# Softmax division moved to tokens on partitions, in a transformer stack of four gated layers on one core

## The reference, cut to what matters

```python
for l in range(4):
    x = x + tanh(g_xattn[l]) * xattn_l(layernorm(x), ctx)
    x = x + tanh(g_ffn[l]) * ffn_l(layernorm(x))
# attention, as in every layer: H heads of width d
probs = softmax(q @ k.T * scale + bias)      # over 256 keys
out = (probs @ v) per head -> [tokens, 128]
y = out @ Wo
```

## Time and profile before

| | us |
| --- | --- |
| median of three runs | 1080.95 |
| lowest, highest | 1071.59, 1083.82 |
| the profiled execution | 1068.41 |
| its span, first to last instruction | 1066.7 |

### The profile page before, as it was taken

How to read it: one execution, slowest core, us unless ns; L and a number is a source line. 1 busy time by engine, 2 the same in 40 slices (tenths; PEclk the granted TensorE clock), 3 DMA queues, 4 the chain that set the end, 5 groups by cost and what they waited for, 6 DMA issues and landing times.

```text
span 1066.7 us, 19274 instructions
## 1 busy us (share of the span) xinstructions
PE 880.5 (83%) x7316; PEld 573.0 (54%) x7316; DVE 787.8 (74%) x1849; ACT 493.7 (46%) x753; POOL 302.4 (28%) x324
## 2 busy tenths in 40 slices
PE   1778787788899998887898877787888999998686
PEld 1533346454566676663465323564456667776443
DVE  3899998778666945449778999878779574554783
ACT  2655453345534532217874656234554343322475
POOL 3600246443443211100323023655335330110000
PEclk9999777698989999988999989677998999988899
DMA  9100000000000000000110000000000000000000
GB/s 322 33 2 2 2 1 1 1 2 2 2 1 2 2 1 6 6 1 2 42 32 21 2 2 1 1 1 2 3 3 1 1 2 1 1 1 1 2 7 17
DMA packets 11741, 14.26 MB, mean 13 GB/s; under 512 B 1604, under 2 KB 10716, under 8 KB 11396
## 3 DMA queue, kind: packets, MB, share of 16 engines
q1 hardware_dynamic: 11552, 12.88, 3.7%
q10 hardware_dynamic: 100, 0.14, 0.1%
HBM read 11.55 MB, written 1.05 MB: 12 GB/s over the span
## 4 chain that ended last, share of the span: by engine, by line
PE 43%; DVE 40%; ACT 7%; issue 6%; SPq 1%; DMA 1%; POOL 1%; DVEq 0%; ACTq 0%
PE banks L986 36%; DVE nm_row L1440 13%; DVE probs L1459 5%; PE pv L986 4%; ACT probs L943 2%; DVE qf_row L1470 2%; DVE wide L1529 2%; DVE st_row L1283 2%; PE banks L682 2%; DVE xn_row L1395 1%; DVE mv_row L1285 1%; DMA xn_row<-in_ctx 1%; ACT wide L965 1%; ACT qT_row L860 1%; ACT kT_row L860 1%
## 5 line engine op out<-in xcount | busy, mean ns | idle before, releaser
L1440 DVE TENSOR_REDUCE nm_row<-banks 128x4 f32<-128x1024 f32 (+1 forms) x192 | 210.3, 1128 | 39.2 <-PE banks L986 38.6
L776 POOL TENSOR_TENSOR rstd_row<-rstd_row,neghalf 128x2 f32<-128x2 f32 x66 | 47.6, 721 | 365.8 <-DVE rstd_row L1390 277.8
L943 ACT ACTIVATE probs<-banks 128x1024 f32<-128x1024 f32 (+1 forms) x144 | 128.2, 933 | 36.5 <-PE banks L986 35.9
L986 PE MATMUL banks<-wide,c 128*128 128x256 f32 x512 | 127.9, 406 | 0.0
L986 PE MATMUL banks<-qT_row,kT_row 50*128 50x256 bf16 (+2 forms) x896 | 89.9, 298 | 29.6 <-DVE nm_row L1440 15.6
L986 PE MATMUL pv<-probs,vpad 128*32 128x256 f32 (+1 forms) x1536 | 105.7, 395 | 9.8 <-ACT probs L938 6.6
L986 PE MATMUL banks<-kT_row,qT_row 48*128 48x256 bf16 (+2 forms) x896 | 92.3, 294 | 25.7 <-DVE nm_row L1440 15.7
L986 PEld LDWEIGHTS banks<-wide,c 128*128 128x128 f32 x512 | 101.0, 202 | 18.3 <-issue 0.9
L938 ACT ACTIVATE probs<-probs 128x1024 f32<-128x1024 f32 x64 | 67.5, 1056 | 50.0 <-DVE probs L1459 48.1
L986 PE MATMUL banks<-c,wide 128*128 128x128 f32 x512 | 85.4, 336 | 3.7 <-POOL wide L834 3.7
L986 PEld LDWEIGHTS banks<-c,wide 128*128 128x128 f32 x512 | 79.6, 245 | 8.1 <-issue 6.4
(11 more groups left out here) (220 smaller groups left out, 1585.5 us busy)
## 6 DMA issues: line engine op xcount, KB each, us to landing
c<-in_c SPq DMA_DIRECT2D x1, 2500.0 KB
wide<-in_mask SPq DMA_DIRECT2D x8, 256.0 KB, 2.9
qT_row<-mT_row SPq DMA_DIRECT2D x96, 4.0 KB
c<-in_c SPq DMA_DIRECT2D x1, 1194.5 KB
xn_row<-in_ctx SPq DMA_DIRECT2D x8, 128.0 KB, 3.5
x_row<-in_x SPq DMA_DIRECT2D x8, 128.0 KB, 2.4
late<-in_late SPq DMA_DIRECT2D x2, 512.0 KB, 15.4
out<-x_row SPq DMA_DIRECT2D x8, 128.0 KB, 2.0
```

Of the source, the lines that this page charges most:

```text
L776: return pool.tensor_tensor(t, t, neghalf[:, 0:n], ALU.pow)
L943: act.activation(dst[:, :, 0:w], src[:, :, 0:w], ACT.Exp, scale=1.0 if l == 2 else HD ** -0.5).then_inc(sem["probs"], 1)
L986: return pe.matmul(dst, lhsT, rhs, start=start, stop=stop, **kw)
L1440: V.tensor_reduce(nm[b][:, t, :, 2 * jp:2 * jp + 2], ps[:, :, :, 0:kn], AX.X, ALU.max, negate=True).then_inc(sem["max"], 1)
```

## The change

The division is done with tokens on partitions. In all four layers `o_flip` on TensorE becomes four f32 transposes of 128x128 (two token tiles t by two groups g) from `weighed_sb` into a bank o_ps. VectorE then inverts, with one token on each partition, only the sums themselves: 32 columns in the wide layers (16 heads for each of two tiles), 8 columns in layer 2, into a corner of the buffer qr. It multiplies with the inverse broadcast along the head: in the wide layers two products of 128 columns (one for each place of a head in its strip), in layer 2 one of 256 columns, into qf. A new step `o_turn` follows: TensorE transposes qf back (two transposes of 128x128), and ScalarE copies the 256 columns into oT. `mix` is as before. The matrix `spreads`, its memset, its eight copies, the wait on `setup_zero` and their part of `n_late` are gone. In the plan, the costs are new (`o_flip` PE .75 and DVE .8 for 1.03 and 2.13, `o_turn` PE .42 and ACT .27), and the eight `LEAD` values are others, so that the orders of all engines are planned anew. The diff, cut to its core:

```diff
@@ row_steps
-        out += [("divide", l, row), ("o_flip", l, row), ("mix", l, row)]
+        out += [("divide", l, row), ("o_flip", l, row), ("o_turn", l, row), ("mix", l, row)]
@@
-LEAD = [280.3, 290.2, 324.8, 314.7, 4.7, -4.1, 22.7, 13.6]
+LEAD = [277.9, 316.1, 319.2, 304.8, -11.0, -1.1, 7.7, 22.0]
@@ COST
-        "o_flip": [("PE", 1.03), ("DVE", 2.13)], ("o_flip", 2): [("DVE", 2.13)], "mix": [("PE", .5), ("DVE", .4)],
+        "o_flip": [("PE", .75), ("DVE", .8)], "o_turn": [("PE", .42), ("ACT", .27)], "mix": [("PE", .5), ("DVE", .4)],
@@ starts_after
-                "o_flip": [(of("divide", l), "ACT")], "mix": [(of("o_flip", l), "DVE")],
+                "o_flip": [(of("divide", l), "ACT")], "o_turn": [(of("o_flip", l), "DVE")], "mix": [(of("o_turn", l), "ACT")],
@@ psum_uses
-        "o_flip": [("oT_ps", "one", "oT")] if l != 2 else [],
+        "o_flip": [("o_ps", "one", "o_normed")], "o_turn": [("oT_ps", "one", "oT")],
@@ SP, step consts
-                        sp.wait_ge(setup_zero, 1)
-                        for j in range(2):
-                            for c in range(LANES):
-                                at_row, head = COLS * c + j * (HD + 1), LANES * j + c
-                                sp.dma_start(spreads[at_row:at_row + HD + 1, :], dram["spreads"][head * (HD + 1):(head + 1) * (HD + 1), 0:P]).then_inc(const_in, 16)
@@ ScalarE
+                    if kind == "o_turn":
+                        evac(oT[b][:, :], "oT_ps", bank("oT_ps", s)[:, 0:SEQ], "oT")
@@ TensorE
-                    if kind == "o_flip" and l != 2:
-
+                    if kind == "o_flip":
                         pe.wait_ge(sem["sums"], at("sums", s))
+                        claim(pe, "o_ps", s)
+                        for t in range(NT):
+                            for g in range(2):
+                                n = 2 * t + g
+                                ins = pe.transpose(bank("o_ps", s)[:, n * P:(n + 1) * P], weighed_sb[b][:, g, t * P:(t + 1) * P], ident)
+                        ins.then_inc(sem["o_ps"], 1)
+                    if kind == "o_turn":
+                        pe.wait_ge(sem["o_normed"], at("o_normed", s))
                         claim(pe, "oT_ps", s)
-                        for i, n in enumerate(("o", "r")):
-                            a, w = SPREAD_COLS[n]
-                            for g in range(2):
-                                ins = mm(bank("oT_ps", s)[g * w:(g + 1) * w, i * SEQ:(i + 1) * SEQ], spreads[:, a:a + w],
-                                         weighed_sb[b][:, g, :])
+                        for t in range(NT):
+                            ins = pe.transpose(bank("oT_ps", s)[:, t * P:(t + 1) * P], qf[b][:, t, :], ident)
                         ins.then_inc(sem["oT_ps"], 1)
@@ VectorE
                     if kind == "o_flip":
-                        over = qf[b][:, :, :].rearrange("p t d -> p (t d)")
+                        dve.wait_ge(sem["o_ps"], at("o_ps", s))
+                        ps = bank("o_ps", s)
                         if l == 2:
-                            dve.wait_ge(sem["sums"], at("sums", s))
-                            num, den = weighed_sb[b][:, 0, :], weighed_sb[b][:, 1, :]
+                            four = ps[:, :].rearrange("p (t n c d) -> p t n c d", t=NT, n=2, c=MQ)
+                            over = qr[b][:, 0, 0:NT * MQ].rearrange("p (t c) -> p t c", t=NT)
+                            ch.link(V.reciprocal(over, four[:, :, 1, :, 0]))
+                            V.tensor_tensor(qf[b][:, :, :].rearrange("p t (c d) -> p t c d", c=MQ), four[:, :, 0, :, :],
+                                            over[:, :, :, None].to_broadcast([P, NT, MQ, MD]), ALU.mult).then_inc(sem["o_normed"], 1)
                         else:
-                            dve.wait_ge(sem["oT_ps"], at("oT_ps", s))
-                            ps = bank("oT_ps", s)
-                            num, den = ps[:, 0:SEQ], ps[:, SEQ:2 * SEQ]
-                        ch.link(V.reciprocal(over, den))
-                        V.tensor_tensor(oT[b][:, :], num, over, ALU.mult).then_inc(sem["oT"], 1)
+                            strips = ps[:, :].rearrange("p (n c w) -> p n c w", n=2 * NT, c=LANES)
+                            over = qr[b][:, 0, 0:NT * HEADS].rearrange("p (n c j) -> p n c j", n=2 * NT, c=LANES)
+                            dst = qf[b][:, :, :].rearrange("p t (g j c d) -> p (t g) j c d", g=2, j=2, c=LANES)
+                            ch.link(V.reciprocal(over, strips[:, :, :, HD:2 * HD + 2:HD + 1]))
+                            for j in range(2):
+                                n = j * (HD + 1)
+                                ins = V.tensor_tensor(dst[:, :, j, :, :], strips[:, :, :, n:n + HD],
+                                                      over[:, :, :, j, None].to_broadcast([P, 2 * NT, LANES, HD]), ALU.mult)
+                                if j == 0:
+                                    ch.mark(ins)
+                            ins.then_inc(sem["o_normed"], 1)
```

More of the change, by code:

```diff
@@ L227, in starts_after @@
                 "norm": [(of("stats", l), "POOL")],
-                "o_flip": [(of("divide", l), "ACT")] if l == 2 else [],
                 "mix": [(of("plus", l), "POOL")],
@@ L308, in signals @@
                 "q_turn": ["q_ready"], "q_mid": ["q_rest"], "q_low": ["q_stack"],
-                "max": ["max"], "shift": ["shift"], "attend": ["biased"], "o_flip": ["oT"], "mix": ["x_mixed"],
+                "max": ["max"], "shift": ["shift"], "attend": ["biased"], "o_flip": ["o_normed"], "mix": ["x_mixed"],
                 "route": ["logits", "gate_in"] if l == 1 else ["logits", "onehot"], "gate": ["onehot"],
@@ L317, in signals @@
                 "shift_flip": ["shiftT"], "attend": ["probs"] + (["v_placed"] if wide and s[3:] == (0,) else []),
-                "divide": ["sums"], "route": ["gate_exp"], "choose": ["onehotT"] + (["u"] if l == 1 else []),
+                "divide": ["sums"], "o_turn": ["oT"], "route": ["gate_exp"], "choose": ["onehotT"] + (["u"] if l == 1 else []),
                 "inner": ["h0"], "again": ["h1"], "deep": ["ht"]}[kind]
@@ L487, in build @@
         small_parts = sb("small_parts", [3 * E, P + FF], BF16)
-        spreads = sb("spreads", [P, P])
         def W(name):
@@ L589, in build @@
         early_in = ctx.enter_context(nc.semaphore("early_in"))
-        setup_zero = ctx.enter_context(nc.semaphore("setup_zero"))
         setup_act = ctx.enter_context(nc.semaphore("setup_act"))
@@ L635, in turn_before @@
             return ("sums", *ended[i - 1][1:]) if i else None
-        n_late = 16 * (len(LATE_PACKS) + 2 * LANES)
+        n_late = 16 * (len(LATE_PACKS))
         def programs(block):
@@ L757, in _ @@
                 ch = Chain(pool, sem["pool"])
-                pool.memset(spreads[:, :], 0.0).then_inc(setup_zero, 1)
                 pool.memset(neghalf[:, :], -0.5)
```

## The result

The changed kernel takes 1100.6 us, median of four runs from 1099.0 to 1104.7; the kernel before, four runs with them, 1080.5. The ratio of the runs, as it stands on record, is 1.0232 with an interval of 1.0183 to 1.0281, some 25 us; the two medians alone are 20 us apart. The forecast was 12 us the other way.

A forecast was written before the change was run, and what follows sets the result against it. It took no engine as full over the whole span: DVE paces some stretches, PE layer 2's, neither the rest. 10.0 + 8.8 - 0.6 + 1.6 - 9.2 + 1.5 = 12.1 us gained, 1069 us on the runs' scale, range 1050 to 1092.

The forecast's parts named there:

- the 11.2 of the sum: TensorE's added work from swapping products for transposes: 1.1 us in wide layers, 10.1 us in layer 2.
- The end of 0.15 us a transpose: Low end for TensorE's transposes, taken from the spread products' busy time; said to make 5.8 us less in all.
- PE's share of the chain above DVE's by more than 3 points: Sign of a right forecast, in the chain of waits that ended last; before, PE had 43% and DVE 40%.
- 1.5 forecast: At the start, eight fewer SP issues let constant packs and context loads land sooner: 1.5 us gained, ends 0 and 3.2.
- A: 8 x 1.25 = 10.0, counted in full: Stretches 53 to 160 and 587 to 693 us, VectorE 97% and 95% busy: its saving counts whole, 10.0 us.
- B: 14 x 1.25 = 17.5, counted at half: Stretches where PE and DVE hand work to each other, neither full: half of VectorE's saving counts, 8.8 us.
- rival 2: Saved VectorE time turns idle because PE is the engine behind: 4.3 us slower, 1085 on the runs' scale; chance 0.22.
- A wide division costs PE 0.045 us more: Wide layers: six transposes for four products add 0.045 us of TensorE time, 24 times, 1.1 us.
- I take wide layers at nothing (shorter by 0.8, longer by two handovers): Path of one wide division: 3.4 us becomes 2.6, against extra turns through PE and ScalarE; priced at no change.
- 9.2 us of PE work: Layer 2's added transposes in stretches where PE sets the pace: 10.2 us counted at 0.9, 9.2 us lost.
- rival 3: Layer 2's division waits twice in PE's queue behind large products: 15 or 30 us, 1099 at 30; chance 0.12.
- Rival 4: TensorE's granted clock falls from 0.902 to 0.85, costing 23 us, 1092; sign: mean clock under 0.88; chance 0.06.

The follow-up runs named there:

- p1: The changed kernel pinned to the engine orders of the kernel before, with only the new turns inserted; 1100.9 us, 1.0291 of before.
- p3: Kernel before, in its own order, with the new division in layers 0, 1 and 3 only; 1084.0 us, 1.0070 of before.
- x3: p3 measured again on another chip: new division in the wide layers only, both turns, order of before; 1.0030 of before.
- r1: Kernel before, orders and turns unchanged, its reciprocal cut to 32 of 256 columns (8 in layer 2), most of the division left out; 0.9928 of before.
- r2: Kernel before with four transposes replacing the wide layers' spreading products, VectorE's operations unchanged and no turn back; 1.0002 of before.
- x1: p3 without the second turn: wide layers' products go straight into oT, transposes back and ScalarE's copy left out; 0.9924 of before.
- t2: Kernel before plus six unread transposes ahead of layer 2's output product, 8 times; 1080.6 us, 1.0052 of before.
- x2: p4 without the second turn: layer 2's product goes straight into oT, transposes back and copy left out; 1.0165 of before.
- p5: p4 with layer 2's inserted turns moved by -1.5 to +12 us of plan time to shorten waits; 1086.7 us, 1.0110 of before.
- p4: Kernel before, in its own order, with the new division in layer 2 only; 1.0139 of before.
- s1: The changed kernel with the eight leads of the kernel before and the new costs; 1115.4 us, 1.0405 of before.

## Why the prediction was wrong

**What held.** The durations: 0.350 for 0.353, 0.285 for 0.286, 0.198 for 0.203, and transposes at 0.186 for 0.21. DVE came to 754, not 746: 69.6 us left and 25.1 came, and DVE's other operations took 11 us more, which was not followed up. PE came to 908.6, not 892: the exchange cost 6.5 us for the 11.2 of the sum, and the rest is the same instructions taking longer. (The end of 0.15 us a transpose would have made the sum's term 11.5 us less, 192 x 0.06, not 5.8; at the measured 0.186 it is 4.6 less.) PE's share of the chain above DVE's by more than 3 points, named as a sign of being right, came true by 11 points in a slower kernel, so it was no sign. SP issued the packs at 6.29 us instead of 7.65, once the issues of the earlier trace rows were gone, and in p1 and p3 the first division comes 2.7 us earlier than before, against 1.5 forecast; in x3, the same kernel as p3, it comes 0.8 us earlier.

**The step that failed first: "A: 8 x 1.25 = 10.0, counted in full ... B: 14 x 1.25 = 17.5, counted at half".** By those shares r1 should have given 22 us; it gave 7.7, with 10.9 as the interval's far end. A alone, counted in full, would have made 11.2 of it. An engine at 95 to 97% over a stretch was taken for the bound of that stretch. The chain had said less: 2% of the span, 21 us, for all 56 us of L1470. DVE waited 39.8 us more for PE in r1, for 42.7 us of saved work: the time turned idle. This is rival 2's mechanism, given 0.22.

**The second: "A wide division costs PE 0.045 us more" and "I take wide layers at nothing (shorter by 0.8, longer by two handovers)".** The sum set the products that leave the first turn against the transposes of both turns. The runs price the two apart: 12.7 us less PE work in the first turn gave nothing (r2, at a slightly lower clock), while the turn back costs 13.5 us (x3 over x1), 0.56 us a division, more than the saved DVE time was worth. 11.1 us of PE work stand in that turn; the two handovers, PE waiting for DVE and ScalarE for PE, were not priced at all. Which of the two costs the time stays open, as said above.

**The third: layer 2 in the sum at 9.2 us of PE work, its waits only as rival 3.** The work costs 5.6 us (t2), less than charged; with the turns it is 15 to 19 us in the order of before, and by x2 the first turn brings all of it, as far as the intervals tell. Rival 3 had the place and the engine, and a chance of 0.12. Its size, 15 to 30 us beside the work, was too large: the runs leave 9 to 13. That its 1099 us stands beside the measured 1100.6 is luck, since 3 to 8 us of the loss are the wide layers', which its sum had gaining. Its reason against, "the plan knows the turns", holds in part: in the changed kernel's own order DVE never waits at the layer 2 reciprocal (0.0 us in its row), but layer 2's maxima (L1432, before L1435) wait 27.8 us for 11.2. As the order is another, it is not shown that the same wait moved there; p5 shows such a move in a fixed order.

**Rival 4, the clock.** It fell: 0.880 against 0.890 in the runs of the changed kernel again and of before beside it; the four runs of the result average 0.8785, under the 0.88 that was named as its sign. Within the kernel before alone, on four chips, the runs lose 3.6, 5.1, 5.4 and 7.2 us per 0.01 of mean clock, fitted by straight lines; if that is the clock's own effect, which such a fit doesn't show, 0.010 is 4 to 7 us. In layer 2 it is hardly the cause: p4 averages 0.888 beside before's 0.890, and its one run at 0.900 took 1090.95 us, where before took 1074.95 at 0.897. In the wide layers it may be most of the small loss (p3: 0.010 lower and 7.5 us, x3: 0.006 lower and 3.2). Part of the loss, not the main of it.

**The sum as the runs have it**, in the order of before: DVE's time -8, the turn back in the wide layers +13, layer 2 +15 to +19, together +20 to +24. p1, with everything, stood 29 us above before, so the parts do not quite add; the changed kernel, in its own order, 23 to 25. How much of that is an order that could be better was not settled: the old leads are worse for it (s1), and no better order for all four layers was found. No kernel here that computes the division beats the kernel before.

## What to carry to other kernels

Before trading one engine's time against a round trip through others, take the time away alone and measure what it is worth; here a kernel with the long reciprocal cut short, 0.7% faster, would have shown that 42 us of VectorE could pay for almost nothing. Don't set work that leaves one place against work that comes in another: here 12.7 us less of TensorE's work gave nothing, and a turn with 11.1 us of it cost 13.5. When a new wait shows up on an engine, look for the wait that it replaces in the same queue, and for the idle time of the engine that is waited for, before you call it the loss: 47 us of it could be taken from one line and stood 40 us larger at the next. And compare edits under one pinned order: an order fitted to one division cost the other 0.6 to 6.3%, more than many edits are worth.

## What was not expected of the hardware

Two-pass f32 products with an identity cost 65% more TensorE time than transposes (45.3 for 27.5 us), and the kernel was not measurably slower (1.0100, interval 1.0047 to 1.0154, for 1.0070, interval 1.0034 to 1.0105), with the granted clock at 0.898 instead of 0.880. And executions of the unchanged kernel before on one chip spread over 1.5% (1067.6 to 1083.1 us) with clocks between 0.880 and 0.910: a single profiled execution of such a kernel can stand 1% off its median, as the one behind the earlier trace rows did.
